# Queries turned by VectorE instead of TensorE in a fused linear-attention and expert block

## The reference

```python
h = layernorm(x) * (1 + ca) + sa                 # ca, sa, ga, ...: six vectors from silu(c) @ wmod
q = elu(h @ Wq.T + bq) + 1                       # 16 heads of 32
k = elu(h @ Wk.T + bk) + 1
v = h @ Wv.T + bv
KV = einsum('bhsd,bhsm->bhmd', k, v)
Z = 1 / (einsum('bhsd,bhd->bhs', q, k.sum(axis=2)) + 1e-6)      # one number per row and head
attn = einsum('bhsd,bhmd,bhs->bshm', q, KV, Z)
x = x + ga * (attn @ Wo.T + bo)
h = layernorm(x) * (1 + cb) + sb
V = h @ fWv.T + fbv                              # value rows
s = ln(V @ Wg.T + bg) + sigmoid(alpha) * ln(norms of the probes Wp)    # 8 experts
w = softmax(top 2 of s)
x = x + gb * (V + sum over experts of w_e * (silu(V @ W1[e].T + b1[e]) @ W2[e].T + b2[e]))
```

## Time and profile before

| | us |
|---|---|
| median of the runs | 1349.24 |
| lowest | 1348.2 |
| profiled execution | 1348.24 |
| its span, first to last instruction | 1346.5 |
| PE busy | 1283.0 (95%) |
| PEld busy | 1064.8 (79%) |
| DVE busy | 962.3 (71%) |
| POOL busy | 545.7 (41%) |
| ACT busy | 535.7 (40%) |

### The profile page before, as it was taken

How to read it: one execution, slowest core, us unless ns; L and a number is a source line. 1 busy time by engine, 2 the same in 40 slices (tenths; PEclk the granted TensorE clock), 3 DMA queues, 4 the chain that set the end, 5 groups by cost and what they waited for, 6 DMA issues and landing times.

```text
span 1346.5 us, 19934 instructions
## 1 busy us (share of the span) xinstructions
PE 1283.0 (95%) x6334; PEld 1064.8 (79%) x6334; DVE 962.3 (71%) x2191; ACT 535.7 (40%) x1093; POOL 545.7 (41%) x397
## 2 busy tenths in 40 slices
PE   8999999999999999998799999999999999999998
PEld 7777877788888888886687878788787878887787
DVE  7877888766666666667577776777777677777764
ACT  2443444544444444443323333333333333343431
POOL 1433333444334444443435344453535445353531
PEclk8998999999999999999899999999999999999999
DMA  6542111112111111112211221212122121212201
GB/s 213 180 143 71 47 48 47 63 62 62 55 55 61 62 62 62 62 47 71 79 61 68 75 94 48 95 55 87 59 83 85 58 94 53 89 56 87 70 25 47
DMA packets 57467, 99.13 MB, mean 74 GB/s; under 512 B 9656, under 2 KB 9784, under 8 KB 57392
## 3 DMA queue, kind: packets, MB, share of 16 engines
q1 hardware_dynamic: 57392, 98.20, 21.9%
HBM read 64.63 MB, written 33.55 MB: 73 GB/s over the span
## 4 chain that ended last, share of the span: by engine, by line
PE 66%; DVE 14%; issue 8%; POOL 3%; ACT 0%; DMA 0%; POOLq 0%; ACTq 0%; DVEq 0%
PE ps L1349 20%; PE ps L1350 20%; PE ps L1354 20%; DVE den_eps L1149 4%; PE ps L1548 4%; DVE qf L1224 3%; DVE den L1146 3%; DVE qT_lo L1198 2%; PE ps L1462 1%; POOL xn_lo L587 1%; POOL ks_acc L583 1%; PE ps L1540 1%; POOL rstd L578 0%; DVE rsq L1242 0%; DVE zf L1238 0%
## 5 line engine op out<-in xcount | busy, mean ns | idle before, releaser
L619 POOL TENSOR_TENSOR cn<-c,half 128x16 f32<-128x16 f32 x32 | 104.2, 3255 | 288.1 <-DVE c L1215 288.1
L578 POOL TENSOR_TENSOR rstd<-veps,neg_half 128x1 f32<-128x1 f32 x64 | 35.1, 549 | 281.4 <-DVE veps L845 281.4
L583 POOL TENSOR_TENSOR ks_acc<-ks_acc,kf 128x512 f32<-128x512 f32 x64 | 82.9, 1295 | 102.3 <-DVE kf L1102 102.3
L587 POOL TENSOR_TENSOR xn_lo<-xn,xn_hi 128x512 fp32r<-128x512 f32 x64 | 110.3, 1724 | 8.9 <-ACT xn_hi L722 8.9
L1108 DVE TENSOR_TENSOR k_lo<-kf,k_hi 128x512 fp32r<-128x512 f32 x64 | 75.5, 1180 | 43.7 <-ACT k_hi L717 36.4
L1349 PE MATMUL ps<-v_hi,xT_hi 128*128 128x512 f32 x256 | 106.3, 415 | 0.0
L1349 PE MATMUL ps<-wk_hi,xT_hi 128*128 128x512 f32 x256 | 106.0, 414 | 0.0
L1349 PE MATMUL ps<-g_hi,qT_hi 128*128 128x512 f32 x256 | 105.0, 410 | 0.0
L1349 PE MATMUL ps<-k_hi,xn_hi 128*128 128x512 f32 x256 | 103.4, 404 | 1.5 <-DVE bq_row L1021 1.5
L1349 PE MATMUL ps<-wq_hi,xT_hi 128*128 128x512 f32 x256 | 103.2, 403 | 0.1
L1350 PE MATMUL ps<-g_lo,qT_hi 128*128 128x512 f32 x256 | 101.6, 397 | 0.0
(11 more groups left out here) (241 smaller groups left out, 3384.7 us busy)
## 6 DMA issues: line engine op xcount, KB each, us to landing
xin<-_attn_hidden_states_dram SPq DMA_DIRECT2D x64, 256.0 KB, 2.8
q_scratch<-qf SPq DMA_DIRECT2D x64, 256.0 KB, 2.9
xin<-_attn_hidden_states_dram SPq DMA_DIRECT2D x32, 512.0 KB, 4.9
q_in<-q_scratch SPq DMA_DIRECT2D x32, 512.0 KB, 4.0
out_dram<-qf SPq DMA_DIRECT2D x64, 256.0 KB, 2.1
wm_in<-in_L_wmod_dram SPq DMA_DIRECT2D x4, 1024.0 KB, 7.4
wm_in<-in_L_wmod_dram SPq DMA_DIRECT2D x4, 512.0 KB, 5.9
raw_k<-in_L_attn_Wk_dram SPq DMA_DIRECT2D x1, 1024.0 KB, 9.3
```

The lines of the kernel that those rows point to most:

```text
L583: nc.gpsimd.tensor_tensor(ks_acc[:], ks_acc[:], kf[:, s, :], ALU.add).then_inc(ks_done, 1)
L587: nc.gpsimd.tensor_tensor(xn_lo[:, 1 - s, :], xn[:, 1 - s, :], f32(xn_hi[:, 1 - s, :]), ALU.subtract).then_inc(xnl_done, 1)
L619: nc.gpsimd.tensor_tensor(cn[:].rearrange("p h e -> p (h e)"), c2[:].rearrange("p h e -> p (h e)"), half[:], ALU.pow).then_inc(cn_done, 1)
```

## The change

The queries are read back so that the 32 partitions i hold columns 128i to 128i+127: for each of four column quarters one transfer brings, for row t of every block of 32 rows, 128 values. Two halves of 128 rows are eight such blocks, so q_in is still 128 x 1024. One VectorE transpose instruction, which transposes every 32x32 block in place of its 32 partitions, then gives both halves in the layout that TensorE needs as its stationary operand, in a new SBUF tile qTf. The rows of that layout stand in another order than before (quarter, then 32 columns within a block), and so Wo, bv, the turned Wv and the KV operands are loaded or written in that order. turn_q and its waits are gone from TensorE. qT_high reads qTf; qT_low moves from VectorE to the end of GpSimd's step. The addition of 1e-6 becomes a ScalarE instruction, and the reciprocal (inverses) moves one step later on VectorE, to just before scaled_q. ks_q holds the sum of k by quarters, made by four small copies. Some tiles that only the preparation uses now share memory with tiles of the second sweep.

```diff
--- before.py
+++ after.py
@@ -92,6 +92,11 @@
+def strided(ap, j):
...
+    return ap.rearrange("p (i j d) -> p i j d", i=KB, j=KB)[:, :, j, :]
@@ -212,6 +217,8 @@
         ks_row = sb("ks_row", [P, D], F32, late)
+        ks_q = sb("ks_q", [P, P], F32, late)
+        qTf = sb("qTf", [P, 2, D], F32, late)
         g_hi = sb("g_hi", [P, KB, D], F32R, late)
@@ -481,10 +489,16 @@
                 if i == 1:
-                    for row, src in ((bv_row, bv), (bo_ga, bo), (fbv_row, fbv)):
+                    for row, src in ((bo_ga, bo), (fbv_row, fbv)):
                         row_load(row[:], src, rows_in)
+                    for b in range(KB):
+                        sp.dma_start(bv_row[:, b * P:(b + 1) * P].rearrange("p (i d) -> p i d", d=DH),
+                                     bv.rearrange("(a i j d) -> a j i d", a=1, i=KB, j=KB)[:, b].to_broadcast([P, KB, DH])).then_inc(rows_in, 16)
                 if i == 2:
-                    sp.dma_start(raw_o[:], Wo.rearrange("(r p) f -> p r f", p=P)).then_inc(o_in, 16)
+                    for r in range(KB):
+                        for b in range(KB):
+                            sp.dma_start(raw_o[:, r, b * P:(b + 1) * P].rearrange("p (i d) -> p i d", d=DH),
+                                         strided(Wo[r * P:(r + 1) * P, :], b)).then_inc(o_in, 16)
                 if i == 4:
@@ -512,9 +526,10 @@
             def q_load(j):
-                wait_count(sp, q_back, 16 * j)
-                sp.dma_start(q_of(j).rearrange("p (h d) -> p h d", d=D),
-                             q_dram[pair_rows(j), :].rearrange("(h p) d -> p h d", p=P)).then_inc(q_back, 16)
+                wait_count(sp, q_back, 64 * j)
+                for i in range(KB):
+                    sp.dma_start(q_of(j)[DH * i:DH * (i + 1), :].rearrange("p (n f) -> p n f", f=P),
+                                 q_dram[pair_rows(j), i * P:(i + 1) * P].rearrange("(n t) f -> t n f", t=DH)).then_inc(q_back, 16)
@@ -605,13 +620,21 @@
             nc.gpsimd.memset(ws[:], 0.0).then_inc(b_cleared, 1)
-            pool.wait_ge(ks_row_done, 1)
+            pool.wait_ge(ksq_done, KB)
...
             def q_times_ks(j):
-                pool.wait_ge(q_back, 16 * (j + 1))
+                pool.wait_ge(q_back, 64 * (j + 1))
                 wait_count(pool, den_done, j)
-                nc.gpsimd.tensor_tensor(qks[:], q_of(j).rearrange("p (h d) -> p h d", d=D), ks_row[:].unsqueeze(1).to_broadcast([P, 2, D]),
+                nc.gpsimd.tensor_tensor(qks[:].rearrange("p h (g f) -> p (h g) f", f=P),
+                                        q_of(j).rearrange("p (n f) -> p n f", f=P),
+                                        ks_q[:].unsqueeze(1).to_broadcast([P, 2 * KB, P]),
                                         ALU.mult).then_inc(qks_done, 1)
...
+            def qT_low(j, h):
+                t = 2 * j + h
+                pool.wait_ge(qTh_done, t + 1)
+                wait_count(pool, o_psum, t - 1)
+                nc.gpsimd.tensor_tensor(qT_lo[:, h, :], qTf[:, h, :], f32(qT_hi[:, h, :]), ALU.subtract).then_inc(qTl_done, 1)
@@ -645,6 +668,9 @@
                     router_scale(j - 1)
+                if live(j + 1, J):
+                    qT_low(j + 1, 0)
+                    qT_low(j + 1, 1)
@@ -670,8 +696,11 @@
                         act.wait_ge(prep_psum, JOB[j] + 1)
-                        dst = wvT[:, b, :] if j[0] == "v" else catT[:, b, :]
-                        nc.scalar.copy(dst, bank(j)[:, 0:dst.shape[1]]).then_inc(prep_taken, 1)
+                        if j[0] == "v":
+                            nc.scalar.copy(wvT[:, b, :].rearrange("p (j i d) -> p i j d", i=KB, j=KB),
+                                           bank(j).rearrange("p (i j d) -> p i j d", i=KB, j=KB)).then_inc(prep_taken, 1)
+                        else:
+                            nc.scalar.copy(catT[:, b, :], bank(j)[:, 0:C]).then_inc(prep_taken, 1)
                     elif j in ("ga", "gb"):
@@ -729,7 +758,9 @@
             for b in (2, 3):
-                nc.scalar.activation(mt[b], ps[:, b, :], ACT.Copy, scale=ca1_col[:, b:b + 1]).then_inc(mt_act, 1)
+                nc.scalar.activation(mt[b].rearrange("p (j i d) -> p i j d", i=KB, j=KB),
+                                     ps[:, b, :].rearrange("p (i j d) -> p i j d", i=KB, j=KB), ACT.Copy,
+                                     scale=ca1_col[:, b:b + 1]).then_inc(mt_act, 1)
             for b in range(KB):
@@ -742,10 +773,15 @@
                 t = 2 * j + h
-                act.wait_ge(qT_psum, t + 1)
+                act.wait_ge(qT_done, j + 1)
                 wait_count(act, o_psum, t - 1)
                 wait_count(act, qTl_done, t - 1)
-                nc.scalar.copy(qT_hi[:, h, :], bank_qaT).then_inc(qTh_done, 1)
+                nc.scalar.copy(qT_hi[:, h, :], qTf[:, h, :]).then_inc(qTh_done, 1)
...
+            def den_plus_eps(j):
+                act.wait_ge(den_done, j + 1)
+                wait_count(act, zr_done, j)
+                nc.scalar.activation(den_eps[:], den[:], ACT.Copy, bias=1e-6).then_inc(deneps_done, 1)
@@ -813,7 +849,10 @@
+                if live(j + 2, J):
+                    den_plus_eps(j + 2)
...
+            den_plus_eps(0)
             sweep_pairs(step_b, -1, J + 1)
@@ -1124,15 +1163,21 @@
             for b in (0, 1):
-                nc.vector.tensor_scalar(mt[b], ps[:, b, :], ca1_col[:, b:b + 1], None, ALU.mult).then_inc(mt_dve, 1)
+                nc.vector.tensor_scalar(mt[b].rearrange("p (j i d) -> p i j d", i=KB, j=KB),
+                                        ps[:, b, :].rearrange("p (i j d) -> p i j d", i=KB, j=KB),
+                                        ca1_col[:, b:b + 1], None, ALU.mult).then_inc(mt_dve, 1)
...
             nc.vector.tensor_copy(ks_row[:], bank("ks")).then_inc(ks_row_done, 1)
+            for i in range(KB):
+                quad = slice(DH * i, DH * (i + 1))
+                nc.vector.tensor_copy(ks_q[quad, :], bank("ks")[quad, i * P:(i + 1) * P]).then_inc(ksq_done, 1)
             dve.wait_ge(ks_row_done, 1)
+            heads = headmask[:].rearrange("p (i d) -> p i d", d=DH)
             for b in range(KB):
-                blk = slice(b * P, (b + 1) * P)
-                last = nc.vector.scalar_tensor_tensor(out=outer[:, b, :], in0=ks_row[:, blk], scalar=bvp_col[:, b:b + 1],
-                                                      in1=headmask[:], op0=ALU.mult, op1=ALU.mult)
+                last = nc.vector.scalar_tensor_tensor(out=outer[:, b, :].rearrange("p (i d) -> p i d", d=DH),
+                                                      in0=strided(ks_row[:], b), scalar=bvp_col[:, b:b + 1],
+                                                      in1=heads, op0=ALU.mult, op1=ALU.mult)
             taken_by(last, "ks")
@@ -1143,14 +1188,14 @@
                 dve.wait_ge(qks_done, j + 1)
+                wait_count(dve, deneps_done, j)
                 nc.vector.tensor_reduce(den[:].rearrange("p h n -> p (h n)"), qks[:].rearrange("p h (n d) -> p (h n) d", d=DH),
                                         AX.X, ALU.add).then_inc(den_done, 1)
-                dve.wait_ge(den_done, j + 1)
-                nc.vector.tensor_scalar(den_eps[:], den[:], 1e-6, None, ALU.add).then_inc(deneps_done, 1)
...
+            def inverses(j):
                 dve.wait_ge(deneps_done, j + 1)
@@ -1171,7 +1216,7 @@
                 dve.wait_ge(zr_done, j + 1)
-                wait_count(dve, qT_psum, 2 * j)
+                wait_count(dve, qT_done, j)
                 nc.vector.tensor_tensor(
@@ -1192,10 +1237,11 @@
-            def qT_low(j, h):
-                t = 2 * j + h
-                dve.wait_ge(qTh_done, t + 1)
-                nc.vector.tensor_tensor(qT_lo[:, h, :], bank_qaT, f32(qT_hi[:, h, :]), ALU.subtract).then_inc(qTl_done, 1)
+            def turned_q(j):
+                dve.wait_ge(qz_done, j + 1)
+                wait_count(dve, qTl_done, 2 * j)
+                nc.vector.transpose(qTf[:].rearrange("p h (j g t) -> p h g j t", j=KB, g=KB),
+                                    qz[:].rearrange("p h (g j f) -> p h g j f", g=KB, j=KB)).then_inc(qT_done, 1)
@@ -1306,10 +1352,13 @@
                 if live(j + 1, J):
+                    inverses(j + 1)
                     scaled_q(j + 1)
...
                     gated(j - 1)
+                if live(j + 1, J):
+                    turned_q(j + 1)
                 if live(j, J):
@@ -1325,14 +1374,10 @@
                     variances(j - 1)
-                if live(j + 1, J):
-                    qT_low(j + 1, 0)
                 if live(j - 1, J):
...
                     x2T_low(j, 0)
-                if live(j + 1, J):
-                    qT_low(j + 1, 1)
@@ -1412,7 +1457,7 @@
                         pe.wait_ge(acc_step, 3 * KB)
-                        pe.wait_ge(rows_in, 48)
+                        pe.wait_ge(rows_in, 96)
                         bank_free(pe, j)
@@ -1425,7 +1470,7 @@
                     elif j[0] == "o":
```

(39 more changed lines are left out.)

## The result

The changed kernel takes 1399.52 us (median of 4 runs, 1397.5 to 1400.17) beside 1348.72 for the kernel before: **slower, ratio 1.0377, interval 1.0357 to 1.0397**. The profiled executions have spans of 1398.5 and 1346.5 us, and mean granted clocks of 0.963 and 0.990. I forecast 1357. The time lies in the range I gave, but it is that of a rival, "slower by the clock"; the forecast itself had +8 us, and +51 came.

A forecast was written before the change was run, and what follows sets the result against it. TensorE sets the pace, stopped once per 21.51 us pair by a VectorE chain whose den_eps waits for GpSimd. Profiled 1348.24, +7 for 30 pairs, +1 between sweeps = 1356; the median lies 1.0 higher: 1357 us, range 1300 to 1402.

The forecast's parts named there:

- slower by the clock: Rival, chance 0.22: TensorE's wait before turn_x2(j,1) lowers its clock, 1.8 us lost; 1411 in every pair, 1384 in half.
- TensorE's floor, 19.41 us per pair: Second sweep: what TensorE would need per pair without the stop and without the two turns of q, 19.41 us.
- The transposition, 1.2 us, hidden: VectorE's new 128x1024 transposition before residual(j,0) takes about 1.2 us, fitting in idle time ahead of residual(j,1); costs nothing.
- the rival of two passes: Rival, chance 0.12: VectorE's transposition takes two passes (2.4 us), up to 1.0 us more per pair, 1387.
- L1238 inherits den_eps's wait: VectorE's variances: with den_eps gone, this 128x16 operation waits for GpSimd instead, ending 0.03 us after xb ends.
- s2 and s3 wait out GpSimd's two qT_low: VectorE's scores: both small operations wait for GpSimd, delaying x2T_low and turn_x2(j,1); pair 0.24 us longer, +7 over 30.
- the one on the clock: Wait before turn_x2(j,1): clock loss decided between waits of 1.70 and 2.81, predicted wait 2.15; forecast charged nothing.
- Thirty pairs alike: Second sweep: 30 of its 32 pairs counted alike, each 0.24 us longer, +7 us.
- Transfers, 0: Query loads split in four and Wo into sixteen loads: nothing charged, bound 5 us once.
- Between the sweeps, +1: Four 32x128 copies for ks_q before the first q_times_ks: 0.8 to 2.7 us together, 1 taken.
- The first sweep, 0: First sweep: the sum had no term for it, so no added time.
- the gain comes through: Rival, chance 0.2: small operations slip past GpSimd or scores run first, x2T_low not late; 1288, half of it 1320.

The follow-up runs named there:

- experiment 4: Changed kernel with x2T_low(j, 0) put ahead of scores(j - 1) in VectorE's order, qT_low staying on GpSimd: 1287.03 us, ratio 0.9555.
- Experiment 6: Buffer addresses only: kernel before with the change's buffer order, 1352.32 us; x2T_low-first kernel with buffers 3360 bytes below old places, 1290.03, or 45056 below, 1282.61.
- experiment 3: Changed kernel with qT_low back on VectorE at its two former places, the rest of the change kept: 1313.6 us, ratio 0.9749.
- experiment 2: Changed kernel with two filler matmuls, results unread, on TensorE just before turn_x2(j, 1): 1375.09 us, ratio 1.0206.
- experiment 1: Changed kernel with ten filler matmuls, results unread, on TensorE just before turn_x2(j, 1): 1368.74 us, ratio 1.0165.

## Why the prediction was wrong, step by step

*TensorE's floor, 19.41 us per pair*: right. 19.31 to 19.40 where nothing stops it (experiments 4 and 6).

*The transposition, 1.2 us, hidden*: right. It takes 1.24, and residual(j,1) still waits 1.02 for TensorE behind it. The Trainium skill ("VectorE: DVE Perf Modes", The three transpose paths) led to an estimate of 2.5 us for it; the trace has 1.24 for 128x1024 in fp32, so the measurement decides against the estimate, and the rival of two passes falls.

*L1238 inherits den_eps's wait* (now L1284): right, 0.03 after xb's end, and rrs ends 1.79 after xb's end where I had 1.78.

*s2 and s3 wait out GpSimd's two qT_low*: right, 1.28 and 1.18 us. x2T_low ends 6.01 after xb's end, where I had 5.95, TensorE waits 2.29 instead of 2.15 and the pair is 21.82 instead of 21.75. Over 30 pairs that is 9 us instead of 7. The Trainium skill ("SBUF — State Buffer", SBUF: two separate sides) says that GpSimd and a VectorE operation with two SBUF inputs exclude each other for a whole instruction, whichever starts first; these rows agree, to 0.03 to 0.08 us. In the other direction the agreement is looser: rrs in experiment 3 ends 0.88 us after VectorE's qT_low, and takes 1.02 by itself.

**The step that failed is the one on the clock**: "It decides somewhere between waits of 1.70 and 2.81, and mine is 2.15". The forecast charged no loss of clock at all, and gave 0.22 to a loss. Measured, the fall costs 1.54 us where it comes, and it comes in 20 of 28 pairs and in the last but one: 21 x 1.54 = 32 of the 51 us. Two things were wrong. First, between 1.70 and 2.81 I had no row, though the trace of the kernel before has one, from its first sweep: a single wait of 1.99 us, shorter than mine, then matmuls of one column, and the clock at its lower level from 81.4 to 84.8 us.
```profile
78.50 0.38 PE L1384 MATMUL ps<-ones,acc_v 128*128 128x1 f32 x2 [1.99 <-DVE acc_v L897]
```
```profile
81.00:85.00 4.00, 4.00 (x14) 3.19 (x14) 2.56 (x8) 1.88 (x3) 1.57 (x2) 0.57 0.14 25
```
It is not the same case as mine, as the matmuls behind it are tiny, but it warns that a wait under 2.15 can be followed by a fall. Second, I looked for one size of wait that decides, and the size alone does not: falls come after 6 of 28 waits of 1.84 to 1.88 (experiment 2) and after 20 of 28 of 2.25 to 2.32, and after one of 2.50 at 683.64 in experiment 3 the clock stays at 1.00. What tells the pairs that lose from those that don't stays open here. The rival did name half of the pairs (1384); two thirds of the price was a better forecast than nothing. The price I gave, 1.8 a pair, was near. The Trainium skill ("TensorE: Matmul & The Clock Gate", HAM oscillation) tells of a kernel whose every tile starts at half clock after its wait; the trace now agrees for 20 pairs of 28. That 1399.5 falls inside a range that ends at 1402 is in part luck: the range left out the clock in nearly every pair, and the first sweep's 5.3 us were in no part of it.

*Thirty pairs alike*: not quite. In the kernel before the last two of them are short (20.3 and 19.25); in the changed one they are not (21.8 and, at full clock, 20.74). That is 2.4 us more than 0.31 for each.

*Transfers, 0*: right. The sixteen Wo loads and the four for each pair stop nothing that lasts: at tile 15 the first sweep is 0.1 us behind the kernel before.

*Between the sweeps, +1*: from the last ks_acc to the first rrs it is +2.7, but only +0.3 (53.43 us) in the run with ten fillers, of which none is issued yet there, and +0.2 with x2T_low first; over the seven kernels with the change in them that stretch takes 53.27 to 56.01. The four copies take 1.23 us together. What differs is where the clock falls. From the windows of the kernel after, and of the one with ten fillers:
```profile
645.00:655.00 10.00, 6.06 (x17) 4.88 (x18) 7.78 (x10) 1.49 (x4) 5.85 (x3) 0.66 0.57 157
```
```profile
645.00:655.00 10.00, 7.48 (x27) 6.07 (x28) 6.35 (x9) 2.35 (x6) 5.88 (x3) 0.83 0.58 157
```
The changed kernel and the one with ten fillers issue the same instructions up to there, so 2.3 of the 2.7 us are not the change's. That the clock accounts for all of the 2.3 is argued, not shown.

*The first sweep, 0*: wrong, +5.3. I left the moved allocations out of the sum, without a reason. Experiment 6 shows that they are the cause.

*The rival "the gain comes through"*: its number, 1288, is what experiment 4 gives (1287), though not for its reason. Nothing slips past GpSimd; the order has to be changed.

## What to carry to other kernels

When an operation moves to GpSimd, look at which small VectorE operations with two SBUF inputs will meet it, and put whatever TensorE waits for ahead of them: two lines exchanged were worth some 110 us here, where the whole change had lost 51. A recurring wait of about 2 us on TensorE has two prices, the wait and the clock after it; weigh the second by a share of the times, not by yes or no, and look in the trace at hand for every wait near that size before you call it free. And when a buffer order changes, compare a stretch whose instructions did not change: its rate may have moved.

## What the runs showed that I had not expected

TensorE's rate hangs on where buffers lie in SBUF. With the same instructions, clock 1.00 and TensorE always busy, 36 tiles take 312.55 us with qf, xin, xn, xT_hi, xT_lo at their old places or 45056 bytes below them, and 316.88 with them 3360 or 48416 below, 1.4% more; wq_hi and what follows it lay at the same addresses in all four. ks_acc is not the buffer: in the run with the old rate it still lay 36128 bytes below its old place, as in experiment 4. The matmuls on k_hi, k_lo and xn_hi, which didn't move, are slower too: 392 and 394 ns on average between 400 and 600 us of the kernel after, 390 in the kernel before. Which buffer and which engine's access does it, and whether the period is 2048 or 4096 bytes, stays open.

More work on an idle TensorE made the kernel some 30 us faster (experiment 1).
